# Decoder kernel, layer 1: twelve instead of eight of a batch's sixteen one-hot groups stand beside the first attention, four instead of eight beside the second

## The reference

```python
def _L1_xattn_ref(x_q, x_kv, indices, W_q, W_kv_down, W_kv_up, W_out):
    ...
    q = (x_q @ W_q.T).reshape(b, nq, H, HD)
    c_kv = x_kv @ W_kv_down.T
    c_sel = c_kv[jnp.arange(b)[:, None, None], indices]
    kv = (c_sel @ W_kv_up.T).reshape(b, nq, K, 2, H, HD)
    k = kv[:, :, :, 0]
    v = kv[:, :, :, 1]
    scores = jnp.einsum('bqhd,bqkhd->bqkh', q, k) * SCALE
    attn = jax.nn.softmax(scores, axis=2)
    out = jnp.einsum('bqkh,bqkhd->bqhd', attn, v).reshape(b, nq, d)
    return out @ W_out.T
```

## Time and profile before

| | |
|---|---|
| median of three runs | 2456.16 us |
| profiled execution, its own time | 2450.69 us |
| its span (first to last instruction) | 2448.8 us |
| PE busy | 2108.3 us (86%) |
| DVE busy | 1317.0 us (54%) |
| ACT busy | 1001.5 us (41%) |
| mean granted TensorE clock | 0.912 of full speed |
| L2918, comparisons | 1024 instructions, 212.2 us busy |
| L2936, counting matmuls | 1024 instructions, 136.5 us busy |

### The profile page before, as it was taken

The page is one execution under the profiler, slowest core; times in us unless marked ns, Lnnn a source line. Parts: engine busy times, 40 slices in busy tenths (PEclk is TensorE's granted clock), DMA queues, the critical chain, the costliest instruction groups (busy, mean ns, idle before and its releaser), DMA issues. The chain is left out here.

```text
span 2448.8 us, 38848 instructions
## 1 busy us (share of the span) xinstructions
PE 2108.3 (86%) x13495; PEld 1499.7 (61%) x13495; DVE 1317.0 (54%) x3919; ACT 1001.5 (41%) x3152; POOL 382.3 (16%) x655
## 2 busy tenths in 40 slices
PE   8678988998999988896637789899999999999875
PEld 4356666665777755775514566666666666666554
DVE  7245576576444364322127567666666666657441
ACT  3123655645453434351212345544444444444321
POOL 2044253262423042001000000000000000000000
PEclk9767999998998988997958899999999999999988
DMA  8000000002222111545750000000000000000000
GB/s 320 5 5 5 6 10 6 10 13 84 94 87 87 46 38 40 184 177 178 204 168 18 2 11 5 6 5 28 5 28 5 28 5 24 5 23 5 22 18 26
DMA packets 56299, 124.79 MB, mean 51 GB/s; under 512 B 9312, under 2 KB 31584, under 8 KB 52256
## 3 DMA queue, kind: packets, MB, share of 16 engines
q1 hardware_dynamic: 54128, 110.13, 13.7%
q10 hardware_dynamic: 432, 7.89, 0.8%
q0 software_dynamic: 1536, 4.20, 0.6%
HBM read 98.59 MB, written 23.59 MB: 50 GB/s over the span
## 5 line engine op out<-in xcount | busy, mean ns | idle before, releaser
L702 ACT ACTIVATE PRS<-PT 128x384 f32<-128x384 f32 (+1 forms) x512 | 266.1, 520 | 572.5 <-PE PT L633 572.5
L767 DVE TENSOR_REDUCE negmax<-SM 128x2 f32<-128x512 f32 x432 | 283.8, 686 | 219.1 <-PE SM L596 208.2
L633 PE MATMUL PT<-const_sb,PRS 128*128 128x128 f32 x1664 | 297.7, 295 | 55.9 <-ACT PRS L702 51.7
L717 ACT ACTIVATE PRS<-SM,negmax 128x128 f32<-128x128 f32 x608 | 248.1, 420 | 160.5 <-DVE negmax L767 158.3
L633 PEld LDWEIGHTS PT<-const_sb,PRS 128*128 128x128 f32 x1664 | 197.2, 148 | 149.7 <-issue 98.3
L2918 DVE TENSOR_SCALAR arena<-arena 128x256 bf16<-128x256 bf16 x1024 | 212.2, 283 | 8.9 <-PE SC L2936 7.9
L586 PE MATMUL SM<-haloU,QM 32*128 32x128 f32 (+1 forms) x1056 | 156.2, 354 | 4.4 <-ACT PRS L717 2.6
L2936 PE MATMUL SC<-arena,identb 128*128 128x256 bf16 x1024 | 136.5, 275 | 8.8 <-DVE arena L2918 8.8
L648 PE MATMUL OA<-PRS,big 128*32 128x256 f32 (+1 forms) x1024 | 131.9, 382 | 1.0 <-ACT PRS L702 0.7
L586 PEld LDWEIGHTS SM<-haloU,QM 32*128 32x128 f32 x1056 | 120.0, 202 | 17.1 <-issue 7.9
L715 ACT ACTIVATE PRS<-SM,negmax 128x256 f32<-128x256 f32 x256 | 105.3, 472 | 47.6 <-DVE negmax L767 29.6
(11 more groups left out here) (593 smaller groups left out, 3997.1 us busy)
## 6 DMA issues: line engine op xcount, KB each, us to landing
arena<-lay SPq DMA_DIRECT2D x50, 1024.0 KB, 4.9
arena<-shares SPq DMA_DIRECT2D x64, 128.0 KB, 2.9
rows<-OT SPq DMA_DIRECT2D x2, 3456.0 KB
arena<-lay ACTq DMA_DIRECT2D x1, 5265.5 KB, 24.3
arena<-lay SPq DMA_DIRECT2D x1, 3862.0 KB, 20.3
arena<-rows SPq DMA_DIRECT2D x25, 128.0 KB, 2.4
arena<-lay SPq DMA_DIRECT2D x25, 128.0 KB, 5.6
rows<-arena SPq DMA_DIRECT2D x25, 128.0 KB, 4.3
```

Source lines behind the costliest of these rows:

```text
L633: ins = pe.transpose(bank[:, o:o + P], PR[n % 4][:, t, k * P:(k + 1) * P], ident)
L702: act.activation(dst, src, ACT.Copy).then_inc(S("probs_moved"), 1)
L717: ins = act.activation(dst, src, ACT.Exp, bias=negmax[:, h, r:r + 1], accum_out=rsum[:, t, h:h + 1])
L767: st.post(dve.tensor_reduce(negmax[:, ORDER[s], :], two(banks[s % NB]), AX.X, ALU.max, negate=True), S("max_ready"))
```

## The change

```diff
         GROUPS_HOT = TT * NI // 8
-        HOT, HOT_FIRST, FEED_FIRST, FEED_PART = GROUPS_HOT + 3, 10, 2, 8
+        HOT, HOT_FIRST, FEED_FIRST, FEED_PART = GROUPS_HOT + 3, 14, 2, 8
```

## The result

The changed kernel takes 2500.97 us (median of four runs, 2500.70 to 2521.33); the kernel before took 2452.18 us beside it (2446.94 to 2458.87). The ratio is 1.0216, with a 95% interval of 1.0178 to 1.0255: slower, and whether by more than 2% stays open. Ratios in this document are estimated from all runs but the slow ones (over 1.5% above the fastest run of the same kernel), so they are not exactly quotients of the medians. The profiled execution took 2500.82 us, its span is 2499.0 us, and its mean granted clock 0.904 where before had 0.912.

A forecast was written before the change was run, and what follows sets the result against it. Tally and count were both taken as close to TensorE's own work. Work +36.9 and clock +10.5 gave +47.4 us: 2498 from the profiled 2450.7, 2503 by the runs' median, stated as 2500; range 2468 to 2522.

The forecast's parts named there:

- Step 1: Slot 0 of tally: group 0 is compared before the row maximum of pair 1, delaying pair 2's scores; +1.6 us.
- Step 3: Slot 5 of tally: TensorE's second group waits 3.45 us for VectorE's same-slot comparisons, plus the group 0.99; +4.4 us.
- Step 5: Slot 7 of tally: TensorE waits 1.6 us for the comparisons of group 9, plus the group 1.0; +2.6 us.
- Slots 2 and 6: In tally, slot 2's second group costs +1.0 us without a wait; slot 6's earlier waits go, -1.5 us.
- Step 6: Slots 8 and 9 of tally: the 1.07 us wait before the last group is filled; -1.1 us.
- Count: Seven count stages lose four groups, 4.0 us of TensorE work, but gain only 1.3 us each; bounds 0 and 4.0.
- Tally(1) and tally(2): These stages lack feed-forward steps, so slot 5 waits only 1.9 to 2.9 us; +5.5 us each.
- The clock: A clock fall behind slot 5's wait in each of seven tally stages, 1.5 us each; +10.5 us, bounds 0 and 28.
- A: Rival: slot dependency real, but its waits come out of existing ones, no clock fall; +14, 2465 to 2470 us; chance 0.14.
- C: Rival: TensorE bounds count and regains 4.0 us a stage, tally costs 0.6; -24, 2427 us; chance 0.06.
- D: Rival: nothing to see, count's gains meet tally losses of about the same size; 2450 to 2462 us; chance 0.08.
- B: Rival: the clock falls longer or in both places, 28 us; +65, 2516 to 2521 us; chance 0.15.

The follow-up runs named there:

- Experiment 3: One-hot steps put first in each slot of tally: in the changed kernel (14 steps) 2480.20 us, in the kernel before (10 steps) 2420.12 us.
- experiment 2: The changed kernel with unused matmuls put ahead of the waiting groups in slots 5 and 7 of tally; 2480.59 us, ratio to before 1.0105.
- experiment 4: Each side alone on the kernel before: four groups left out beside count, 2437.06 us; tally as changed with count as before, 2512.42 us.

## Why the prediction was right, and where it was off

Forecast 2500, measured 2500.97, slower, by the mechanism named. That the two agree to 1 us is luck, since errors of opposite sign cancel, as the end of this list shows. The terms, each by what the traces show:

- **Step 1, slot 0 (+1.6).** From pair 1 to pair 2 tally(5) grew by 1.55 us. VectorE compares before the row maximum, and the next scores wait 0.80 us. After:

```profile
1939.57 1.66 DVE L2918 TENSOR_SCALAR arena<-arena 128x256 bf16<-128x256 bf16 x8
1941.15 1.28 DVE L767 TENSOR_REDUCE negmax<-SM 128x2 f32<-128x512 f32 x2
...
1943.63 0.92 PE L586 MATMUL SM<-KF,QM 32*128 32x128 f32 x8 [0.80 <-ACT PRS L717]
```

- **Step 3, slot 5 (+4.4).** The wait is 3.43 us (forecast 3.45), scores to scores +4.49. Experiment 3 took VectorE's other work out of the wait, and it fell to 0.37.
- **Step 5, slot 7 (wait 1.6).** 1.84 us; the whole slot +3.67 in tally(5), with a fall in it.
- **Steps 1 to 5 together** were +8.1. At a clock of 1.00 the stage is 64.02 us in experiment 2 and 55.93 before: +8.09. Slots 2 and 6 (+1.0, -1.5) are in this sum; alone they read -0.64 and -0.2, since a fall of before went from the one and one of after reaches into the other.
- **Step 6 (-1.1)** lies behind the OA copy, so in the stretch of the next count.
- **Count (-1.3 a stage).** At 1.00 the kernel before has 65.64 us. Less 1.3 and less the 1.1 of step 6 makes 63.24, which is the length of count(4) after. Slot by slot, in the kernel after:

```profile
2009.95 1.13 PE L586 MATMUL SM<-AM,haloU 32*128 32x256 f32 x8 [0.43 <-ACT PRS L715]
...
2023.67 1.13 PE L586 MATMUL SM<-AM,haloU 32*128 32x256 f32 x8 [0.99 <-ACT PRS L715]
...
2052.73 0.63 PE L633 MATMUL PT<-const_sb,PRS 128*128 128x128 f32 x4 [1.57 <-DVE PRS L774]
```

In slots 3 and 7 the place of the removed group is now a wait, 0.99 us before pair 4 and 0.68 + 0.9 = 1.57 before the flips: nothing gained, as the earlier trace rows let one expect.

- **Tally(1) and tally(2), +5.5 each.** The waits of slot 5 are 1.80 and 2.83 us (forecast 1.9 to 2.9). Work grew by 4.2 and 4.7: about 1 us too high in each. Work in all was forecast as +36.9 and is +32.7.
- **The clock, +10.5: this term was mis-sized; it is +21.7.** I had priced one fall behind the wait of slot 5 in each of seven stages at 1.5 us, and none in slot 7. The trace of the kernel after, read in stretches of 0.2 us, has a fall at the wait of slot 5 in tally(2) to tally(7) and none in tally(1) (wait 1.80). The six cost 1.7, 1.7, 3.4, 3.4, 3.4 and 5.1 us (half their length), 18.8 in all against 10.5: the price was too low, and it is not one price. Against that, the falls of before at pair 2 in tally(4) to tally(7), 1.7 us each, are gone.

In slot 7 the same wait of 1.84 us came with a fall in tally(4) and tally(5), 1.7 us each, and with none in tally(3), tally(6) and tally(7). The waiting group in tally(3), then in tally(4), both after:

```profile
1727.26 1.06 PE L2936 MATMUL SC<-arena,identb 128*128 128x256 bf16 x8 [1.84 <-DVE arena L2918]
...
1857.62 1.89 PE L2936 MATMUL SC<-arena,identb 128*128 128x256 bf16 x8 [1.84 <-DVE arena L2918]
```

Last, I looked for falls only where a wait was added. By the table of stages count(0) lost 5.4 us and tally(2) 7.0 us more than before by the clock, 12.4 in all (the counts from 1 to 6 lost 4.9 less than before): count(0) behind a wait that had a group in it, and tally(2) half behind its slot 5 and half behind waits of 1.24 and 0.67 us near its start, which the change did not touch and which cost 1.7 us before.

So a work term 4 too high, a clock term 11 too low, and 5 us by which the unchanged part ahead was shorter made a total that is nearer to the result than its parts were. 54.4 - 4.6 = 49.8 us, and the forecast was 47.4.

The page TensorE: Matmul & The Clock Gate of the Trainium skill (section Terms), which counts a throttled stretch at its length times one minus the granted share, would have made that term 22 us by the seven stretches assumed, and by the same count it is 21.7. The agreement is in the sum only: the falls are not the seven that were assumed. By experiment 2 this count is a little high: it has 3.3 us for tally(5), and filling the waits gave back 2.85.

Of the rivals, A is out: the waits of before did take up 1.5 + 1.1 us of a stage, but no more. C is out by experiment 4. D is out by both the size and the waits at L2936. B had the direction of the clock term right: the falls of slot 5 cost more, and others came in more places. Its 28 us were too many.

## What to carry to other kernels

When two engines step through slots and the consumer runs one group behind the producer, a second group in a slot turns a distance of one slot into none. Price it as the time from the consumer's arrival to the end of all that stands ahead of the producer's group in that slot, and add the row maxima or the like that the doubled step pushes back. Ask also of each group that leaves a stage whether it stood in a wait: if so it gains nothing, and its place may become a wait behind which the clock falls. Where the order inside a slot is free, putting the producer's step first gave 1.45% here with one step to a slot; with two steps in some slots it moved one wait to an earlier slot and left another.

## What the runs showed of the hardware

- How long TensorE waits does not by itself tell whether its clock falls. In the kernel after it fell at waits of 3.43 us in all five stages from tally(3) on and at waits of 1.84 us in two stages of five; at 2.17 us in count(0) it fell in all five kernels that have this wait. In the kernel before it fell in tally(5) with no wait longer than 0.67 us in the 9 us ahead (0.67 us up to 1907.10 and 0.23 up to 1909.35). The stretch behind, in which TensorE is busy throughout and granted 0.57:

```profile
1909.35:1912.80 3.45, 3.45 (x21) 1.86 (x21) 3.45 (x13) 1.32 (x5) 0.00 (x0) 0.57 0.21 73
```

- Not every fall has a wait ahead of it. In count(3), count(4) and count(5) of the kernel before the clock fell though TensorE had not waited in the 10 us ahead. It did so 1.2 to 1.4 us after sixteen matmuls of 128x8 (L2976, 1.85 us); the same run in count(2) was followed by none.
- Unused matmuls in the waits kept the clock at 1.00 in tally(3) to tally(7), and the kernel gained 20 us by them.
- Fewer falls can pay for more work: with 11 steps in tally the layer had 13.8 us more work than before and was 2.2 us shorter.
- With the same instructions ahead of it, the first score matmul of layer 1 started between 1366.3 and 1389.7 us from one profiled execution to the next, and the kernel before took 2428.5 to 2478.5 us in 25 runs. A difference of under 10 us between two single executions says nothing here.
